# Wider sums on GpSimd, casts moved to ScalarE, a shorter prefix and half-width group steps in a three-layer kernel

## The reference, cut to what matters

```python
attn = softmax(einsum('bnchw,bncyx->bnhwyx', q, k) / sqrt(C))
x = x + out_w @ einsum('bnhwyx,bncyx->bnchw', attn, v)
t = tokens(x);  z = ln(t);  d = z - mean16(z);  u = d / (std16(d) + 1e-5)
k, v = kw * u + kb, vw * u + vb
t = t + z + z @ (k^T v / N)
z = ln(t);  p = softmax(z @ gate_w + gate_b);  t = t + sum over the top 2 experts of p_e * ffn_e(z)
```

## Time and profile before

| | us |
|---|---|
| median of 3 runs | 2252.08 (2238.56 to 2256.55) |
| profiled execution, its own time | 2246.34 |
| its span, first to last instruction | 2244.6 |
| PE, DVE, POOL, ACT busy | 1754.7, 1379.7, 1434.8, 1071.3 |

### The profile page before, as it was taken

One profiled execution on the slowest core, in us unless ns is written; L12 is line 12 of the kernel. 1 busy time (PEld: TensorE's weight loads), 2 busy tenths in 40 slices (PEclk: granted clock), 3 DMA queues, 4 the chain that ended last, 5 costly groups with the idle time before them and its releaser, 6 DMA issues.

```text
span 2244.6 us, 38139 instructions
## 1 busy us (share of the span) xinstructions
PE 1754.7 (78%) x11103; PEld 884.2 (39%) x11256; DVE 1379.7 (61%) x3701; ACT 1071.3 (48%) x1898; POOL 1434.8 (64%) x1779
## 2 busy tenths in 40 slices
PE   5999898897888989798898978885337677777744
PEld 2233333332333333333333333333326566566632
DVE  5677878686776768677686866754434333333345
ACT  1565655555455555545455555452115444444432
POOL 1777587875968678596877769676335555555530
PEclk8999999998988999799898999896568888887865
DMA  2220220211202022120202112010323333322259
GB/s 64 57 57 12 55 81 17 76 37 51 77 14 84 15 76 53 38 77 21 76 13 75 47 44 73 6 38 31 101 76 119 107 115 96 93 76 75 74 150 319
DMA packets 130824, 155.20 MB, mean 69 GB/s; under 512 B 19678, under 2 KB 93170, under 8 KB 130688
## 3 DMA queue, kind: packets, MB, share of 16 engines
q1 hardware_dynamic: 113408, 117.76, 18.9%
q0 software_dynamic: 16896, 35.69, 4.7%
q10 hardware_dynamic: 384, 0.00, 0.0%
HBM read 65.03 MB, written 55.84 MB: 54 GB/s over the span
## 4 chain that ended last, share of the span: by engine, by line
PE 49%; issue 14%; DVE 12%; another core or an unknown queue 8%; POOL 6%; ACT 5%; SPq 4%; DMA 1%; DVEq 0%; ACTq 0%; POOLq 0%
PE psum L1573 8%; PE psum L1620 7%; PE psum L1593 7%; PE psum L1683 6%; DVE rowmax L1198 5%; PE psum L1670 5%; PE psum L1554 3%; PE psum L1421 3%; POOL probs L624 2%; PE psum L1428 2%; PE psum L1576 2%; PE psum L1659 2%; PE psum L1458 1%; POOL arena L624 1%
## 5 line engine op out<-in xcount | busy, mean ns | idle before, releaser
L1198 DVE TENSOR_REDUCE rowmax<-psum 128x1 f32<-128x512 f32 x1024 | 670.1, 681 | 304.3 <-PE psum L1620 184.9
L1620 PE MATMUL psum<-arena 128*128 128x512 bf16 x872 | 332.9, 405 | 103.8 <-DVE rowmax L1198 81.1
L797 ACT ACTIVATE probs<-psum 128x1024 f32<-128x1024 f32 x256 | 251.1, 1021 | 209.7 <-PE psum L1576 203.5
L797 ACT ACTIVATE arena<-psum 128x1024 f32<-128x1024 f32 x256 | 252.7, 1021 | 179.8 <-PE psum L1576 176.6
L610 POOL DMA_INDIRECT sorted_scratch<-rows,slot_idx x256 | 251.1, 981 | 91.9 <-issue 69.6
L1620 PEld LDWEIGHTS psum<-arena 128*128 128x128 bf16 x1024 | 92.5, 101 | 550.0 <-DVE rowmax L1198 384.9
L1573 PE MATMUL psum<-qk 32*128 32x512 f32 x2048 | 300.6, 657 | 7.9 <-ACT probs L797 4.3
L1683 PE MATMUL psum<-probs 128*128 x1088 | 186.4, 326 | 100.5 <-ACT probs L866 100.4
L624 POOL TENSOR_TENSOR probs<-probs 128x256 f32<-128x256 f32 x352 | 243.7, 729 | 16.5 <-PE psum L1593 13.5
L624 POOL TENSOR_TENSOR arena<-arena 128x256 f32<-128x256 f32 x352 | 243.9, 728 | 13.5 <-PE psum L1593 10.9
L1683 PEld LDWEIGHTS psum<-probs 128*128 128x128 f32 x1088 | 174.9, 236 | 128.9 <-issue 121.6
(11 more groups left out here) (203 smaller groups left out, 2794.3 us busy)
## 6 DMA issues: line engine op xcount, KB each, us to landing
arena<-part SPq DMA_DIRECT2D x256, 128.0 KB, 2.8
qk<-sorted_scratch SPq DMA_DIRECT2D x136, 144.0 KB
probs<-y_scratch SPq DMA_DIRECT2D x64, 256.0 KB, 5.1
x_in<-in_x_dram SPq DMA_DIRECT2D x16, 512.0 KB, 3.5
x_res<-in_x_dram SPq DMA_DIRECT2D x16, 512.0 KB
t_scratch<-t SPq DMA_DIRECT2D x16, 512.0 KB
arena<-t_scratch SPq DMA_DIRECT2D x8, 1024.0 KB
out_dram<-probs SPq DMA_DIRECT2D x32, 256.0 KB, 5.3
```

The source lines that it names most:

```text
L797: a.activation(group[:, 2 * i:2 * i + 2, :].rearrange("p s n -> p (s n)"), st_pair[i], ACT.Exp, scale=float(C) ** -0.5).then_inc(exp_done, 1)
L1198: v.tensor_reduce(rowmax[:, half, kh, h, j:j + 1], ps[:, :], AX.X, ALU.max)\
L1620: t_.matmul(ps[:, :], qs1[:, par, h, qb * P:(qb + 1) * P], ks1[:, par, h, kh * HALF:(kh + 1) * HALF], start=True, stop=True)\
```

## The change

- `sum_pair` makes 4 adds of 512 columns in place of 8 of 256.
- The high parts of q and k are written by ACT, straight from PSUM with the bias, ahead of the float32 copy that it writes anyway; the casts on POOL (L600), and on DVE for image 0, go. ACT waits at `q0` until the stacks of the image before have been read out of `part`.
- `prefix` becomes three adds over all blocks (distance 1, 2, 4) on zero-padded tiles, in quarters 27, 28, 31.
- ACT reads the Gram matrix in place of DVE (four instructions). The head mask is multiplied into the value weights once at the start, and `kv_product` has four steps in place of five.
- `gsum`, `d16`, `ss` and `u` are each done in two halves of 4 blocks; `gsum` in quarters 19 and 20, `ss` in 23 (was 25). The third of four pairs of `z` blocks moves from quarter 20 to 19, the second transposition `zT1` from 27 to 24.
- `slots` and `slot_numbers` do both choices in one instruction each.

```diff
-    'zT1': 27, 'z': (19, 19, 20, 20), 'd16': 20, 'u': 23, 'prefix': (27, 27, 27, 27, 28, 28, 30, 31), 'gsum': 20, 'ss': 25
+    'zT1': 24, 'z': (19, 19, 19, 20), 'd16': (20, 20), 'u': (23, 23), 'prefix': (27, 28, 31), 'gsum': (19, 20), 'ss': (23, 23)
-    PAIRS, SUM_PARTS = 4, 8
+    PAIRS, SUM_PARTS = 4, 4
...
                 pool.wait_ge(raw_ready, 4 * b + c + 1)
-                g.tensor_copy(part[:, 0, which, cols], qk[:, par, which, cols]).then_inc(high_ready, 1)
-                pool.wait_ge(high_ready, parts_made(b, c))
+                pool.wait_ge(high_ready, 4 * b + c + 1)
...
+                    if b > 0 and name == "q0":
+                        for h in range(NH):
+                            act.wait_ge(stacked1[1 - par][h], 16 * STACK1_DMAS * ((b - 1) // 2 + 1))
+                    a.activation(part[:, 0, which, cols], ps[:, :], ACT.Identity,
+                                 bias=bqk[:, which:which + 1]).then_inc(high_ready, 1)
                     a.activation(qk[:, par, which, cols], ps[:, :], ACT.Identity,
                                  bias=bqk[:, which:which + 1]).then_inc(raw_ready, 1)
...
+                elif name == "gram":
+                    ps = from_shared(name, pair, p)
+                    a.activation(usum[:, :], ps[:, C:C + 1], ACT.Copy).then_inc(gram_out, 1)
+                    a.activation(kvw[:, 0, :], ps[:, 0:C], ACT.Copy, scale=kcol[:, 0:1]).then_inc(gram_out, 1)
+                    act.wait_ge(gram_out, 3 * b + 1)
+                    a.activation(udiag[:, :], ident[:, :], ACT.Copy, scale=usum[:, :]).then_inc(udiag_ready, 1)
+                    a.activation(kcc[:, :], usum[:, :], ACT.Identity, scale=kcol[:, 0:1], bias=kb_n[:, :])\
+                     .then_inc(gram_out, 1)
...
+                        for half in (0, 1):
+                            blocks = slice(4 * half, 4 * half + 4)
+                            if q == AT["d16"][half]:
+                                pool.wait_ge(gsum_ready, 4 * b + 2 * half + 2)
+                                g.tensor_tensor(grouped(d16[:, blocks, :]), grouped(z[:, blocks, :]),
+                                                wide16(gsum[:, 1, :])[:, blocks], ALU.subtract).then_inc(d_ready, 1)
+                            if q == AT["u"][half]:
+                                pool.wait_ge(rs_step, 5 * b + 5)
+                                g.tensor_tensor(grouped(u[:, blocks, 0:C]), grouped(d16[:, blocks, :]),
+                                                wide16(rs16[:, 1, :])[:, blocks], ALU.mult).then_inc(u_ready, 1)
...
                     if k == 0:
                         dve.wait_ge(gate_step, 16 * b + 15)
+                        ins = v.tensor_tensor(two_of[:, 2:, :], chosen[:, 1:, :], chosen[:, 0:BLK, :], ALU.add)
+                    elif k == 1:
+                        dve.wait_ge(prefix_step, 3 * b + 1)
+                        ins = v.tensor_tensor(four_of[:, 4:, :], two_of[:, 2:, :], two_of[:, 0:BLK, :], ALU.add)
                     else:
-                        dve.wait_ge(prefix_step, 8 * b + k)
-                    v.tensor_tensor(before[:, k + 1, :], before[:, k, :], lg[:, 8, k, :], ALU.add)\
-                     .then_inc(prefix_step, 1)
+                        dve.wait_ge(prefix_step, 3 * b + 2)
+                        ins = v.tensor_tensor(before[:, 1:, :], four_of[:, 4:, :], four_of[:, 0:BLK, :], ALU.add)
+                    ins.then_inc(prefix_step, 1)
```

More of the change, by code:

```diff
@@ L349, in conv_attention_hybrid_kernel @@
         u_ready = sem("u_ready")
+        gram_out = sem("gram_out")
         kv_step = sem("kv_step")
@@ L924, in _ @@
             v.memset(negm[:, :, :, :], 0.0).then_inc(ones_rows, 1)
-            v.memset(before[:, 0, :], 0.0).then_inc(dve_const, 1)
+            for t in (before[:, 0:1, :], chosen[:, 0:1, :], two_of[:, 0:2, :], four_of[:, 0:4, :]):
+                v.memset(t, 0.0).then_inc(zeros_in, 1)
+            dve.wait_ge(zeros_in, 4)
             dve.wait_ge(bn_step, 2)
@@ L948, in first_parts @@
                     dve.wait_ge(raw_ready, c + 1)
-                    v.tensor_copy(part[:, 0, which, cols], qk[:, 0, which, cols]).then_inc(first_high, 1)
-                    dve.wait_ge(first_high, 2 * c - 3)
+                    dve.wait_ge(high_ready, c + 1)
                     v.tensor_tensor(part[:, 1, which, cols], qk[:, 0, which, cols], part[:, 0, which, cols],
-                                    ALU.subtract).then_inc(first_high, 1)
+                                    ALU.subtract).then_inc(first_low, 1)
             def other_weights():
@@ L957, in other_weights @@
                 v.tensor_scalar(kb_n[:, :], kcol[:, 1:2], float(N), None, ALU.mult).then_inc(dve_const, 1)
+                for j in range(2):
+                    v.tensor_tensor(vrow[:, j, :], vrow[:, j, :], headmask[:, :], ALU.mult).then_inc(dve_const, 1)
                 dve.wait_ge(wT_ps, 4)
@@ L1049, in piece @@
                 b, _, par = image(SHARED[name][1], pair, p)
[L1050 to L1056, removed]
-                     .then_inc(kv_step, 1)
-                elif name[:3] == "t2_":
+                if name[:3] == "t2_":
                     half = int(name[3])
@@ L1179, in slot_numbers @@
             def slot_numbers(b, par):
-                dve.wait_ge(slot_step, 6 * b + 4)
+                dve.wait_ge(slot_step, 4 * b + 3)
                 v.tensor_scalar(token[:, :], token[:, :], float(N), None, ALU.add).then_inc(token_ready, 1)
-                for c in range(2):
-                    v.tensor_reduce(slot_of[:, c, :], slot[:, 1 + c, :, :], AX.X, ALU.add).then_inc(slot_step, 1)
-                dve.wait_ge(slot_step, 6 * b + 6)
+                v.tensor_reduce(slot_of[:, :, :], slot[:, 1:3, :, :], AX.X, ALU.add).then_inc(slot_step, 1)
+                dve.wait_ge(slot_step, 4 * b + 4)
                 v.tensor_copy(slot_idx[:, par, :], slot_of[:, :, :].rearrange("p c k -> p (c k)")).then_inc(idx_ready, 1)
@@ L1236, in iteration @@
                         gate(b, p, [i for i in range(16) if AT["gate"][i] == q])
-                        prefix(b, [k for k in range(BLK) if AT["prefix"][k] == q])
+                        prefix(b, [k for k in range(3) if AT["prefix"][k] == q])
                     if in_range(-1, pair, p):
```

105 lines of the change are left out of this document (52 added, 53 removed).

## The result

The changed kernel takes 2366.98 us (median of 4 runs, 2360.78 to 2369.56) against 2246.77 of the kernel before on the same chip: ratio 1.053, 95% interval 1.048 to 1.058, **slower by 5.3%**. The forecast was 2239, its widest range ended at 2280. The profiled execution took 2369.56 us, its span is 2367.7.

A forecast was written before the change was run, and what follows sets the result against it. PE was taken as the longest list, with 13% stalls and part at the lower clock. Terms +11.6 - 19 + 7 - 4 - 2.5 - 6 = -13 us: 2246.3 to 2233, as median 2239; range 2222 to 2258, with rivals 2206 to 2280.

The forecast's parts named there:

- Part 1: DVE's deviations beside POOL's 512-column sums: each step waits for one POOL add; +11.6 us, bounds 0 and +19.
- Part 4: The rest of DVE's work: nearly all hidden in quarters 27 to 7; what shows was put at -4 and -2.5 us.
- the four steps: DVE's four small steps of deviations for layer 2, quarters 17 to 19: 3.9 us beside 512-column adds.
- Rival B: Longer locks in deviations stall PE in every image, as in the existing long cases: slower, +25 to 2277 us; chance 0.23.
- Part 2, the holds of `values`: Quarters 13 and 17: shorter POOL work starts scatter bursts sooner, so late releases of values shrink; -19 us.
- Part 3, ScalarE's copies: ACT's high-part copies delay the float32 copy after q1, and so PE's denominators, 0.5 us an image: +7 us.
- The Gram steps: After the Gram product, shared_ps is free some 0.5 us sooner, for which PE waited 4.1 us in all: -4 us.
- `u` in halves: DVE's heads and u come 0.34 us sooner, two halves cost +0.17: -0.2 us in 13 images, -2.5 us.
- Rival A: Bursts end before values are due, holds vanish, PE keeps full clock, every image like the shortest: 2208 us; chance 0.27.

The follow-up runs named there:

- e2: The kernel after, with the sums in 8 adds of 256 columns again in place of 4 of 512: 2208.6 us, 0.988 of the kernel before.
- e7: The kernel after with 512-column adds, POOL waiting for its first add in each block before the second: 2228.9 us, 0.995 of the kernel before.
- e8: The kernel before, with one change: ScalarE makes the high parts from PSUM in place of POOL: 1.003 of the kernel before.
- e12: The kernel before, with ScalarE reading the Gram product, the head mask multiplied in ahead of the loop, and DVE's chain of five made four: 0.999 of before.
- e9: The kernel after with 8 adds and the halves (group sums, d, u, squares' sums) whole again: 2205.0 us, 0.987 of the kernel before.
- e10: The kernel after with 8 adds of 256 columns, POOL waiting for each block's first add before the second: 2208.1 us, 0.989 of the kernel before.
- the sweep: No layer computed: POOL's chains of adds behind a scatter, a 64-column DVE step started at swept moments; 9.8 us at 512 columns, at the chain's start.
- e3: The kernel before, with one change: the sums in 4 adds of 512 columns in place of 8 of 256: 2384.6 us, 1.070 of before.
- e4: The kernel before, with one change: the prefix in three 64-column steps in quarters 27, 28, 31 in place of eight of 8: 2224.5 us, 0.998.

## Why the prediction was wrong

**The step that failed** is Part 1's sentence "Each waits for the end of one POOL add", with its upper bound of +19 us. A DVE step that meets 512-column adds directly behind a scatter waits for the end of the chain, and these steps aren't those of `deviations`. The net loss is 120 us, and the lock-out costs about 130: after against e2 is 1.0529 - 0.9881 = 6.5% or 146 us (give or take 20), less the 15 us of the width alone. e7 gives 131 directly, and the steps' own excess of 133.6 us says the same. The rest of the change gives back about 27 (e2).

The warning stood in the profile that I had read: the earlier trace rows show 3.66 us, a wait for five further adds, to the end of the chain (918.31), and the adds there follow a scatter without a gap:

```profile
911.83 0.97 POOL L610 DMA_INDIRECT sorted_scratch<-rows,slot_idx  x1 [0.30 <-issue]
912.81 5.50 POOL L624 TENSOR_TENSOR probs<-probs 128x256 f32<-128x256 f32 x8
```

In the images where they stand behind a gap of 1.2 to 1.3 us, as in the earlier trace rows, the step takes 0.24 us. I priced it as something of four images. I didn't ask what it had in common, nor where else in the image a scatter stands right ahead of adds. Quarters 24 and 25 are such a place, and there the chain is nine instructions long.

**Part 4's "nearly all of it lies in quarters 27 to 7, where PE has no gap: 0"** failed with it. PE had no gap there because the row maxima were in time; nothing was said of what a held DVE instruction would do to them.

**Part 1's size** for the four steps was right, 3.9 us forecast:

```profile
1200.59 0.16 DVE L1049 SCALAR_TENSOR_TENSOR rstd<-rstd 128x8 f32<-128x8 f32 x1
1200.78 1.13 DVE L1051 TENSOR_TENSOR rstd<-rstd 128x8 f32<-128x8 f32 x1
1201.94 1.20 DVE L1053 SCALAR_TENSOR_TENSOR rstd<-rstd 128x8 f32<-128x8 f32 x1
1203.18 1.18 DVE L1055 SCALAR_TENSOR_TENSOR rstd<-mv,rstd 128x8 f32<-128x8 f32 x1
```

They take 3.8 us (against the earlier trace rows), and +11.6 us stands beside 15 measured for the width as a whole. Rival B had the sign right, for the wrong place: it was to lie in the deviations.

**Part 2, the holds of `values`: -19.** POOL's side came as forecast (busy 1434.8 to 1329.3 us; four adds in 4.95), but the holds moved in place of shrinking. The remote wait in ACT's maxima is gone, and one of the same size stands at `t`, ACT's copy of the projected rows (us in total, times, longest):

```profile
ACT t L751 <- remote: 62.6, 14, 5.8
```

In e8, where only the high parts moved to ScalarE, it is the same (71.7 us in 12 cases at `t`, none at the maxima) and the time is not better. So the runs show no gain where the prediction had -19; e8 has only the casts' part of POOL's relief in it, and ScalarE's cost beside it, so no run measures the term by itself.

**Part 3, ScalarE's copies: +7.** The denominators still follow `q1`'s second copy at once:

```profile
1264.66 1.92 PE L1573 MATMUL psum<-probs,ones 128*32 128x512 f32 x16
```

The copy is 1263.93 to 1264.61. e8 costs 0.3% or 6 us, whose interval includes 0; with the relief of POOL in it, it doesn't isolate the 7.

**Part 4's sizes.** The Gram steps: -4 us forecast, e12 gives -0.1%, no difference from either. `u` in halves: -2.5, and e9 shows nothing; PE's wait for `u` was to fall to 2.4 us an image and is 2.9 on average (45.7 us in 16 waits). DVE's busy time, forecast to fall by 60 us or more, rose by 79.0 in the kernel after (1379.7 to 1458.7), with the held steps in it, and fell by 48.6 in e2; ScalarE's rose by 50.7 in the kernel after, 55 forecast. That the parts are worth more together had no place in a sum of terms. Rival A's sum takes 94.1 us for the shortest image, where the earlier trace rows show 93.5; the outcome doesn't hang on it.

**A version that beats both:** e2, the change with 256-column adds, 2208.6 us and 0.988 (0.981 to 0.995); e9 and e10 are as fast within their intervals. With 512 columns and the one wait (e7) it is 0.995.

## What to carry to other kernels

When VectorE works beside GpSimd, look for an indirect DMA on GpSimd with SBUF-reading work directly behind it, and put a wait for its own first instruction there; here it cost 0.2 us a block and took back 130. With 256-column adds there was nothing to take back (e10), so look first whether a step is held. Before the shape of one engine's blocks is changed, list the other engine's instructions that could meet them by their mean time in the groups view: an instruction that takes 0.2 us alone and several beside something, even in a few images, is a mechanism to be explained, not an outlier to be averaged. And a held instruction counts as busy, so compare an engine's busy time with what its work should take.

## What the runs showed of the hardware that I had not expected

- A scatter followed within 0.03 us by 512-column adds that read SBUF shuts VectorE's SBUF steps out until GpSimd's chain ends (9.8 us in the sweep for a step at the chain's start, 10.6 in the kernel after). A step that comes in the fourth add is still shut out, and a one-column instruction without a wait changes nothing; 0.08 us of GpSimd waiting for itself ends it.
- At 512 columns a DVE step that comes in the last 0.66 us of the scatter itself is shut out as well (10.53 us), one that comes 0.81 us or more before the chain is not (0.22). All twelve 11.6 us cases of e3 are of this kind. At 128 columns only the last 0.26 us did this, and at 64 and 192 a step that came there got in (0.53 us at most).
- Nine widths from 64 to 1024 columns lock out, 256 don't. In the full kernels 256-column chains did so now and then, for 3.1 to 3.8 us, always at the first step of `deviations`: of the images in which it met a chain directly behind a scatter, four of five in the kernel before and five of seven in e4. The one of before that got in came 1.90 us into the chain (0.26 us), two that were held came at 1.88 and 1.92. Why 256 differs, and when it doesn't, stays open.
- A copy of 64 columns with one SBUF input is held like an add with two.
